# Reordered opening of a four-layer kernel: x loaded first, VectorE's statistics ahead of its copies, GpSimd normalising half of x, unread products in TensorE's gaps

## What is computed

```python
x = L0_attn_z
xn = _layernorm(x, axis=-1)                 # (x - mean) / sqrt(var + 1e-5)
x = x + _L0_attn_ref(xn, wq, wk, wv, fcq_w, fcq_b, fck_w, fck_b, fcv_w, fcv_b, fco_w, fco_b)
      + _L0_ffn_ref(xn, ...)                # local attention plus routed attention
...                                         # layers 1, 2, 3
```

## Time and profile before

| | |
|---|---|
| median of 3 runs | 1679.22 us |
| lowest, highest | 1674.57, 1681.4 us |
| the profiled execution's own time | 1685.4 us |
| its span | 1683.6 us |
| mean granted TensorE clock | 0.962 of full |
| TensorE busy | 1485.1 us, 88% |
| VectorE, ScalarE, GpSimd busy | 1087.8, 928.6, 648.9 us |

### The profile page before, as it was taken

The page is one execution under the profiler, slowest core; times in us unless marked ns, Lnnn a source line. Parts: engine busy times, 40 slices in busy tenths (PEclk is TensorE's granted clock), DMA queues, the critical chain, the costliest instruction groups (busy, mean ns, idle before and its releaser), DMA issues. The chain is left out here.

```text
span 1683.6 us, 30888 instructions
## 1 busy us (share of the span) xinstructions
PE 1485.1 (88%) x10541; PEld 1030.0 (61%) x10541; DVE 1087.8 (65%) x2724; ACT 928.6 (55%) x2444; POOL 648.9 (39%) x831
## 2 busy tenths in 40 slices
PE   6999999889989998999999895888789876999976
PEld 5667666556666665777777663555457623555544
DVE  4588888875665664565544345777523287999964
ACT  3588888555555563554454441333344348888945
POOL 4799999710000001002220252314424302888820
PEclk8999999999999998999999996999999977999998
DMA  9000000000000003000000114000011121333300
GB/s 293 14 1 14 14 14 27 1 1 1 1 1 1 1 2 117 1 2 17 17 17 24 44 60 170 2 1 13 26 51 57 55 61 39 90 85 85 94 13 26
DMA packets 48433, 65.43 MB, mean 39 GB/s; under 512 B 7839, under 2 KB 34568, under 8 KB 47530
## 3 DMA queue, kind: packets, MB, share of 16 engines
q1 hardware_dynamic: 43738, 54.08, 11.0%
q0 software_dynamic: 4544, 9.38, 1.5%
HBM read 52.86 MB, written 15.77 MB: 41 GB/s over the span
## 5 line engine op out<-in xcount | busy, mean ns | idle before, releaser
L2384 POOL TENSOR_TENSOR weighted<-state,c_all 128x512 f32<-128x512 f32 x128 | 163.6, 1298 | 77.4 <-DVE state L2394 60.8
L943 DVE TENSOR_REDUCE pair_negmax<-psum_all 128x2 f32<-128x512 f32 x192 | 123.4, 684 | 66.5 <-PE psum_all L632 65.6
L770 ACT ACTIVATE probs<-psum_all,pair_shift 128x256 f32<-128x256 f32 x256 | 118.2, 473 | 78.4 <-POOL pair_shift L473 78.0
L2394 DVE TENSOR_TENSOR_SCAN state<-decay,psum_all 128x512 f32<-128x512 f32 x128 | 149.0, 1200 | 14.2 <-PE psum_all L2312 11.4
L770 ACT ACTIVATE probs<-psum_all,pair_negmax 128x256 f32<-128x256 f32 x192 | 88.6, 473 | 105.2 <-DVE pair_negmax L943 56.9
L2021 POOL DMA_INDIRECT found<-values,dest x78 | 74.9, 960 | 154.2 <-ACT values L2014 131.6
L480 POOL TENSOR_SCALAR probs<-probs,pair_recip 128x256 f32<-128x256 f32 x128 | 121.8, 958 | 5.5 <-DVE pair_recip L963 5.5
L781 ACT ACTIVATE probsT<-psum_all 128x512 f32<-128x512 f32 x224 | 122.5, 611 | 0.3 <-PE psum_all L645 0.3
L2322 PE MATMUL psum_all<-weighted,ident 128*128 128x512 f32 x256 | 121.4, 598 | 0.0
L473 POOL TENSOR_SCALAR pair_shift<-pair_negmax,row_term 128x1 f32<-128x1 f32 x256 | 102.9, 417 | 36.7 <-DVE pair_negmax L943 36.6
L645 PE MATMUL psum_all<-ident,probs 128*128 128x128 f32 x896 | 116.7, 273 | 0.1
(11 more groups left out here) (401 smaller groups left out, 3442.0 us busy)
## 6 DMA issues: line engine op xcount, KB each, us to landing
c_all<-c_rows SPq DMA_DIRECT2D x64, 256.0 KB, 3.3
slots<-slot_fill_dram SPq DMA_DIRECT2D x2, 2535.0 KB, 14.3
ring<-slots SPq DMA_DIRECT2D x18, 260.0 KB, 2.9
keys<-found SPq DMA_DIRECT2D x16, 256.0 KB, 4.6
scale_rows<-row_scales SPq DMA_DIRECT2D x8, 256.0 KB, 4.6
up<-up_dram SPq DMA_DIRECT2D x1, 2048.0 KB, 7.7
down<-down_dram SPq DMA_DIRECT2D x1, 2048.0 KB, 12.2
up<-up_dram SPq DMA_DIRECT2D x1, 1408.0 KB, 5.9
```

The costliest lines, as they stand in the source:

```text
L770: nc.scalar.activation(k.probs[:, 2 * (u % PAIR_BUF) + j, t, :], k.psum[score_bank(u, j)][:, SEQ * t:SEQ * (t + 1)], ACT.Exp, bias=shift[: ...
L943: nc.vector.reduce_max(k.pair_negmax[:, u % 2, SUB * j:SUB * (j + 1)], src, AXX, negate=True).then_inc(s.negmax_ready, 1)
L2384: nc.gpsimd.tensor_tensor(w.weighted[:, u % RING, :], w.state[:, u % RING, :], w.c_all[:, u // L3_DC % C_RING, :], ALU.mult)\
L2394: nc.vector.tensor_tensor_scan(w.state[:, u % RING, :], w.decay[:, u % L3_RING, :, :].rearrange("p b n -> p (b n)"), k.psum[u % PARTS_RING ...
```

## The change

Six edits, all in `layer0_stage`:

1. SyncE issues x chunks 1 to 3 right behind ident, ahead of the query and fold factors.
2. VectorE takes the statistics of all four chunks, normalises chunks 0 and 1, and makes the second scales before it saves any job. The `reduce_sum` comes after pair 1 is saved.
3. ScalarE takes all four roots, the second scales' root and the table load behind its save of x_turn, and only then saves query_turn 0, fused 0 and fused 1.
4. GpSimd normalises chunks 2 and 3 only; the row product stands between the two.
5. The semaphore `x_normed` becomes one for each chunk.
6. TensorE gets `keep_running` (two unread products) ahead of row_weights, and behind the late jobs of steps 0, 1 and 2.

```diff
@@ SyncE
                 for dst, src in first_loads:
                     sp.dma_start(dst, src).then_inc(s.first_loaded, 16)
+                for c in range(1, CHUNKS):
+                    sp.dma_start(k.x[:, CT * c:CT * (c + 1), :], x[:, CT * c:CT * (c + 1), :]).then_inc(x_loaded[c], 16)
                 for dst, src in query_loads:
                     sp.dma_start(dst, src).then_inc(s.query_loaded, 16)
                 for dst, src in fold_loads:
                     sp.dma_start(dst, src).then_inc(s.fold_loaded, 16)
-                for c in range(1, CHUNKS):
-                    sp.dma_start(k.x[:, CT * c:CT * (c + 1), :], x[:, CT * c:CT * (c + 1), :]).then_inc(x_loaded[c], 16)
@@ GpSimd
-                pool.wait_ge(s.query_loaded, 16 * len(query_loads))
-                pool.wait_ge(s.fold_loaded, 16 * len(fold_loads))
-                nc.gpsimd.tensor_tensor(w.row_product, w.fc[:, :], w.kbias_rows, ALU.mult).then_inc(s.weighted_rows, 1)
-                for c in range(1, CHUNKS):
+                for c in range(2, CHUNKS):
+                    if c == CHUNKS - 1:
+                        pool.wait_ge(s.query_loaded, 16 * len(query_loads))
+                        pool.wait_ge(s.fold_loaded, 16 * len(fold_loads))
+                        nc.gpsimd.tensor_tensor(w.row_product, w.fc[:, :], w.kbias_rows, ALU.mult).then_inc(s.weighted_rows, 1)
                     pool.wait_ge(s.rstd_ready, c + 1)
@@ TensorE
                 for job in before:
+                    if job == ("row_weights", 0, 0):
+                        keep_running(nc, k, 0, 2)
                     do(job)
...
                     for job in late[u]:
                         do(job)
+                    if u in (0, 1, 2):
+                        wait_saved(pe, ("fused", 0, 1))
+                        keep_running(nc, k, YB, 2)
@@ ScalarE
                 root(0)
                 do(("x_turn", 0, 0))
-                do(("query_turn", 0, 0))
-                root(1)
-                do(("fused", 0, 0))
-                root(2)
-                do(("fused", 0, 1))
-                root(3)
+                for c in range(1, CHUNKS):
+                    root(c)
                 act.wait_ge(s.moments_ready, 2)
                 nc.scalar.activation(w.norm_scale[:, :, :], w.norm_scale[:, :, :], ACT.Sqrt).then_inc(s.scales_ready, 1)
                 nc.scalar.preload_act_table_set("natural_log_exp_and_others")
+                for job in before[1:]:
+                    do(job)
@@ VectorE
                 chunk_statistics(0)
                 chunk_norm(0)
                 chunk_statistics(1)
-                do(("query_turn", 0, 1))
-                do(("keys", 0, 0))
+                chunk_statistics(2)
+                chunk_norm(1)
+                chunk_statistics(3)
+                second_scales()
+                for job in before[1:8]:
+                    do(job)
                 dve.wait_ge(s.weighted_rows, 1)
                 nc.vector.reduce_sum(w.row_sums[:, :], w.row_product.rearrange("p (h e) -> p h e", e=HD), AXX).then_inc(s.row_weights_summed, 1)
-                chunk_statistics(2)
-                for job in before[5:10]:
+                for job in before[8:]:
                     do(job)
-                chunk_statistics(3)
-                second_scales()
```

More of the change, by code:

```diff
@@ L352, in value @@
         return k.values[:, g % 2, kt, HD * h:HD * (h + 1)]
-    with signals(nc, "x_loaded_0", "x_loaded_1", "x_loaded_2", "x_loaded_3", "first_loaded", "fold_loaded", "main_loaded", "weights_loaded", "variance_ready", "rstd_ready", "x_normed",
+    with signals(nc, "x_loaded_0", "x_loaded_1", "x_loaded_2", "x_loaded_3", "first_loaded", "fold_loaded", "main_loaded", "weights_loaded", "variance_ready", "rstd_ready", "x_normed_0", "x_normed_1", "x_normed_2", "x_normed_3",
                  "moments_ready", "scales_ready", "zeroed", "scaled", "query_loaded", "scales_sent", "scales_spread_0", "scales_spread_1", "rows_turned", "weighted_rows", "row_weights_summed", "mask_cast", "null_weighted", "bias_summed", "bias_added", "shift_ready", "pool_normed",
@@ L359, in layer0_stage @@
         scales_spread = (s.scales_spread_0, s.scales_spread_1)
+        x_normed = (s.x_normed_0, s.x_normed_1, s.x_normed_2, s.x_normed_3)
         x_loaded = (s.x_loaded_0, s.x_loaded_1, s.x_loaded_2, s.x_loaded_3)
@@ L413, in _ @@
                         nc.gpsimd.tensor_scalar(k.xn[:, t, :], k.x[:, t, :], k.moments[:, t, 0:1], k.rstd[:, t:t + 1], ALU.subtract, ALU.mult)\
-                            .then_inc(s.x_normed, 1)
+                            .then_inc(x_normed[c], 1)
                 def scale_weights():
@@ L430, in add_bias @@
                     pool.wait_ge(s.bias_summed, 1)
-                    pool.wait_ge(s.x_normed, TILES)
+                    for c in range(CHUNKS):
+                        pool.wait_ge(x_normed[c], CT)
                     rows = k.x[:, SUB * q:SUB * (q + 1), :]
@@ L511, in do @@
                     if what == "x_turn":
-                        pe.wait_ge(s.x_normed, CT * (i + 1))
+                        pe.wait_ge(x_normed[i], CT)
                         for j in range(CT):
@@ L842, in chunk_norm @@
                         nc.vector.tensor_scalar(k.xn[:, t, :], k.x[:, t, :], k.moments[:, t, 0:1], k.rstd[:, t:t + 1],
-                                                ALU.subtract, ALU.mult).then_inc(s.x_normed, 1)
+                                                ALU.subtract, ALU.mult).then_inc(x_normed[c], 1)
                 def second_scales():
```

## The result

The changed kernel takes **1685.31 us** (median of six runs, 1683.97 to 1691.96), the kernel before, measured with it, 1676.66 (1673.15 to 1681.4). The ratio is 1.0053, with an interval of 1.0033 to 1.0073: 5.5 to 12.2 us slower. In the profiled executions the spans are 1690.2 us against 1683.6, clock 0.961 against 0.962.

What follows compares the result with a forecast made beforehand. It took a ring of waits between engines, not one engine, to bound the first steps, in a loop without slack; 5.8 - 0.2 - 0.2 + 0.9 = +6.3 on 1679.2 gave 1685.5 us, range (8 in 10) 1680.5 to 1691.0.

Steps and rivals of the forecast that it cites:

- rival A: Whole kernel, the forecast itself: 5.8 us lost in the opening, kept by the unread products; 1685.5 us; chance 0.42.
- rival B: Opening and steps 0, 1: unread products meet the lower clock, +1.7 or +2.65; one step gives +9.0, 1688.2 us; chance 0.25.
- The opening to fused 0: Layer 0's start: VectorE's statistics, then ScalarE's root and table load, put fused 0 at 16.35 us, against 10.69 before.
- Order of loads: Loads at the start: factors land at about 12 to 12.5 us, covered by 1 us or more; costs nothing.
- From fused 0 to the scores: TensorE from fused 0 to unit 0's scores: first unread pair 1.8 us, just hidden; scores at 26.05, 5.8 late.
- Steps 0 and 1: First two loop steps: 5.7 us each from scores to scores, against 5.95 and 5.86 before.
- Step 2: Third loop step: 8.7 us from scores to scores, against 7.80 before; scores 3 at 46.15, 6.3 late.
- From unit 3 on the change touches nothing: Loop from unit 3's scores on: no further effect; the delay there, 6.3 us, goes to the end one to one.
- has no slack: Layer 0's loop: TensorE works 19.81 of 20 us from 100 to 120 us, so a late start isn't made good.
- C: Opening: VectorE's normalisation 1 and GpSimd's of chunk 2 block each other, +2.0, so +8.3, 1687.5 us; chance 0.05.
- D: Opening: upper clock throughout, fused 0 0.95 shorter and the pairs 1.1; +4.2, 1683.4 us; chance 0.16.
- E: Steps 0 to 2: products fall into waits, steps cost 4.0, 4.0 and 6.9 us; +1.1, 1680.3 us; chance 0.12.

Runs made afterwards that it cites:

- f1_change: The changed kernel again, unedited, on the second chip, against the kernel before: 1686.57 us, ratio 1.0050.
- g3_scalar_early: The change without unread products, ScalarE saving query_turn 0 and fused 0 ahead of the fourth root, second scales' root and table load: 1678.88 us, 1.0014.
- g1_first_pair: The change with only the first two unread products, ahead of row_weights; the six of steps 0 to 2 gone: 1678.34 us, 1.0016.
- f3_doubled: The change with four unread products, not two, behind each late job of steps 0, 1 and 2: 1691.21 us, 1.0078.
- f2_no_products: The change without its eight unread products, on the second chip: 1680.29 us, 1.0019.
- g2_in_waits: Only x chunk 1 ahead of the factors, GpSimd's chunk 3 behind its first shift, plus unread products ahead of instructions that wait: 1672.15 us, 0.9972.
- e2_products_only: The kernel before plus only the change's eight unread products, in the same four places: 1695.63 us, 1.0051.

## Why the prediction was right, and where it was off

The forecast, rival A, said 1685.5 us; it was 1685.31, and the ratio's interval covers +6.3 us. But the agreement is partly luck. The +6.3 was put on 1679.2, the median of three runs; over six it is 1676.66, 2.6 lower, and that offset hides what the sum lacked. The change cost 8.65 us by its own medians and 9.6 by f1_change's, nearer to rival B's +9.0.

*The opening to fused 0: right.* Chunk 1's statistics began at 6.85 with no wait, the last second scale ended at 13.79 + 0.25 = 14.04 (14.0 said), query_turned was saved at 15.62 (15.6), fused 0 started at 16.27 and took 2.07 (16.35, 2.0). The save of query_turned stands 1.29 us behind the start of the table load, as in the earlier trace rows, and the load itself 0.02 behind the end of the root: the drain of 1.4 us that the Trainium skill (ScalarE: Activation LUTs, What ACT_TABLE_LOAD costs) adds to a switch isn't there.

*Order of loads: right in its result, wrong in its margin.* The factors were to be there by 12 to 12.5; the last one landed at 14.40 in the profile of the change. GpSimd lost 0.67 us to it, hidden; TensorE's keys ended 0.69 us before ScalarE's save let fused 0 go. The "cover of 1 us or more" was 0.7 on TensorE, and g3_scalar_early shows it used up.

*From fused 0 to the scores: one term mis-sized.* VectorE's row sums ended at 23.40 (23.35 said). The first unread pair was taken at 1.8 us, "just hidden by the sum"; it took 2.96, 2.53 in f1_change, 3.20 in g1_first_pair, 3.62 in f3_doubled. The step that failed is "TensorE has then worked without a break for 5 us, so I take the upper level", at 0.7 to 1.8 us. Row_weights started at 24.34, not 23.4, and unit 0 at 26.81 (26.29 in f1_change), not 26.05.

*Steps 0 and 1: right at the upper level.* Both came out at 5.73 and 5.72 in f1_change (5.7 said). In the profile of the change step 0 took 7.41, with its pair at 3.55: of rival B's 2.65 us for a step at the lower level that is the 1.7 for the products, while the biases stayed at 1.15.

*Step 2: low by 0.7 to 2.1.* 8.7 was said, 9.42 and 10.79 came: the clock fell behind the wait of 2.15 us ahead of keys, which the step's sum had not asked about.

*"From unit 3 on the change touches nothing": wrong by 1.4 us.* From unit 3 to unit 8 it took 33.6 us in both profiles of the change and 32.2 before, since the scores of unit 3 and those after the next wait again ran at less than the upper level (1.93 and 1.31 us, against 1.13 and 1.14 before). The code is the same there; what is left of the clock is not. That the loop "has no slack" holds within some 2 us: from unit 8 to 111 the difference goes from 11.0 to 11.4, with up to 13.1 between, and in f2_no_products from 4.4 to 3.1.

*The rivals.* B is what the profiles show, with one pair in full and part of another. C is out: normalisation 1 ran beside GpSimd's in 1.08 us, 1.11 alone, and GpSimd's took 3.25, not 3.11. By the shared port rule of the Trainium skill (SBUF — State Buffer, Who interferes with whom) one should have blocked the other for whole instructions, here of 0.78 us, if VectorE's ran in a two-port mode; the trace doesn't name the mode, and no such block is in it. Something smaller is: two of the second scales' instructions, 128x16, took 0.33 and 0.32 us beside GpSimd's, 0.17 each in the kernel before, where GpSimd was idle. D is out, by fused 0. E's steps of 4.0 were seen only without products in the loop: step 1 of f2_no_products (4.00) and step 0 of g1_first_pair (3.98). Its premise, that they would fall into waits, fails by the order on TensorE: the wait is ahead of the late job, and the products are behind it.

*What stays open.* On the first chip the change without its products cost 0.45% (1.0029 to 1.0062), on the second 0.19% (1.0008 to 1.0031), with like marks up to unit 111. The intervals just overlap; whether there is more to it than noise, and where it would lie, no run tells, as there is no profile of the kernel before from that chip. Nor does any run tell what decides the clock of a given step.

## What to carry to other kernels

Work that only keeps TensorE busy is free only ahead of the instruction that waits, and no longer than the wait; behind it, it costs its whole length, here 0.9 us a product, and twice that where the clock is low. That it is free in the wait is what the timeline of g2_in_waits shows; that it gains anything there is not shown. When work is moved to the front of an in-order list, look at what then stands ahead of the first thing another engine waits for: loading and measuring all of x first helped VectorE and GpSimd and put fused 0 back by 5.6 us, while the order that brings only one chunk forward, with GpSimd's last chunk behind its first shift, gained 0.25%. And before a limit is called hidden, measure the distance to the next: here a table load and a late transfer stood 0.7 us apart.

## What was not expected of the hardware

In one of these profiles the granted clock and the length of records disagree early in the span. The first three are stretches of the changed kernel, the last is of f1_change (us, PE, PEld, DVE, ACT, POOL, PEclk, DMA share, GB/s):

```profile
18.00:20.00 2.00, 2.00 (x11) 2.00 (x11) 0.12 (x1) 0.60 (x1) 1.84 (x3) 1.00 1.03 421
32.00:34.00 2.00, 2.00 (x3) 0.41 (x2) 0.00 (x0) 0.00 (x0) 0.00 (x0) 0.51 1.25 433
48.00:50.00 2.00, 2.00 (x6) 0.56 (x6) 0.00 (x0) 0.00 (x0) 0.00 (x0) 0.50 0.00 0
18.00:20.00 2.00, 2.00 (x11) 2.00 (x10) 0.16 (x1) 0.60 (x1) 1.06 (x2) 0.50 1.04 424
```

From 18 to 20 us the changed kernel's says 1.00, the level of 2.4 GHz, though the two pair products took 2.05 us there, against 1.10 at the upper level, and the biases 1.71, against 0.95 in the kernel before. In f1_change the same jobs took the same 1.71 and 2.05, and there it says 0.50, the level of 1.2 GHz. From 32 us on the two agree in the changed kernel too. Where they disagree, the records' length is what the time follows. And the state at the start is not the same in every execution of one kernel: the sixteen records of the query product took 3.78 us in the profile of the change, 2.05 in f1_change.

The clock fell behind waits shorter than I had reckoned with, and not behind each of them: in e2_products_only the biases behind a wait of 1.90 us took 1.85 us, after scores at the upper level; in f1_change values behind a wait of 2.02 us took 0.67, but the scores behind it 1.37 and the turn after them 1.91. In the kernel before a wait of the same 2.02 us, ahead of the same values, was followed by scores in 1.14 us and a turn in 1.04.
